# The expert stage as one program: gates of four batches first, shared tiles next, and the routing arithmetic spread over the first tiles

## The chip, the cores and the metric

The kernel runs on one core of a Trainium2 chip. The time is the device time of one execution in microseconds (us). TensorE is called PE here, VectorE DVE, ScalarE ACT, GpSimd POOL and SyncE SP, as the profile does.

## The reference, cut to what matters

The whole program is a small network: five stages of attention and feed-forward, and last a mixture of experts. Only that last stage is touched:

```
logits = x @ gate_w.T                       # x: 4096 normalized rows of 256
scores = softmax(logits)                    # over 8 experts
topk_w, topk_i = top_k(scores, 2)
topk_w = topk_w / (topk_w.sum(-1) + 1e-20) * 2.5
g = silu(x @ w_gate[e]) * (x @ w_up[e])     # 352 wide
expert_out = g @ w_down[e]
y = sum of the two chosen experts' outputs, each times its topk_w
out = y + (silu(x @ sw_gate) * (x @ sw_up)) @ sw_down    # shared network, 704 wide
```

The result is added to the residual rows.

## The kernel before, in words

The stage is the function `stage_expert_ffn`. It holds the 4096 rows as 32 tiles of 128 rows and 256 columns (`NT = 32`, eight tiles to each of four batches, `TB = 8`). It multiplies with 352-wide networks only: the shared network is cut in two halves, A and B. So there are ten networks of `NW = 2176` columns (gate, up and down side by side), each loaded by one DMA and split in a high part (ACT, `split_high`) and a low part (POOL, `split_low`), since every product is made of high times high, high times low and low times high.

It has two programs (Blocks) with a barrier between them.

**The first program** is the routing. SP saves the residual rows to memory and loads the networks. DVE measures and normalizes the rows (`measure`, `apply`). PE turns each batch (16 transposes, L3353) and multiplies it with the gate (32 small products, L3362). Then 40 small operations run on DVE one after the other. Each is a `step`: DVE waits for its own semaphore before it goes on. They make the softmax, pick the two best experts, count the rows of each expert (with two products on PE, L3368 and L3369, and a running sum over the 32 tiles), and give each row its place (`slots`) in a list that is sorted by expert. ACT makes the exponential in between.

**The second program** is a pipeline over `K = 135` tiles of rows: 0 to 31 are the 32 tiles with shared half A, 32 to 102 are 71 tiles of the sorted list with the expert of each (`R0 = 32`), and 103 to 134 are the 32 tiles with shared half B, where the two expert outputs of each row are gathered and added. In iteration i each engine does, in this order:

- PE: turns the rows of tile i+1 (L3571), `up(i)` (12 products, L3594 to L3599), turns the product of tile i-1 (L3606), `down(i-2)` (9 products, L3617 to L3619).
- ACT: `high_x(i+1)` (L3638), in some tiles a whole `split_high` (L3273), silu of tile i (L3664), `hT_high(i-1)` (L3668).
- DVE: `low_x(i+1)` (L3674), adds of tile i-3 (L3682), the product `prod(i)` of silu and up (L3713), `hT_low(i-1)` (L3716). In iteration 0 it makes the last 8 routing steps too (`place_tiles`, `weigh_picks`).
- SP: loads and stores of the kept rows and of the sorted list.

Each waits for the others by semaphores: silu(i) for up(i) and for prod(i-1), up(i) for prod(i-2), and so on, so that a delay of one is soon a delay of all.

In the same time POOL spreads the rows: 64 indirect DMAs (L3539), each of which writes 128 rows to their places in the sorted list. It makes them in eight bursts of eight, and after each burst it splits one network (704 and 1472 columns, L3277). Tile 32 needs all 64 and all splits:

```
for t in range(NT):
    g.wait_ge(upped.sem, upped.at(3 * t // 4))
    for i in range(2):
        g.indirect_dma_start(xs[:, :], ...)
    if t % 4 == 3:
        split_low(g, t // 4 + 1, 0, GU)
        split_low(g, t // 4 + 1, GU, NW)
```

## Time and profile before

| | |
|---|---|
| median of 3 runs | 4069.13 us (4068.13 to 4070.47) |
| the profiled execution | 4078.57 us, its span 4076.8 us |
| granted TensorE clock, mean of the span | 0.928 |
| PE busy | 3499.0 us (86% of the span) |
| DVE busy | 2930.9 us (72%) |
| ACT busy | 2550.4 us (63%) |
| POOL busy | 1863.8 us (46%) |

The shares are means over six stages. The expert stage is the last 597 us of the span (from 3479.9 to 4076.8 us), and what is said below is read in it, but for one stretch of an earlier stage. Times such as 3552.55 are microseconds from the start of the span.

### The profile page before, as it was taken

The numbers are of one execution on the slowest core, as the hardware profiler recorded it, in microseconds if no ns is written. First come the engines' busy times: TensorE is split into PE (matmuls) and PEld (weight loads), VectorE is DVE, ScalarE is ACT, GpSimd is POOL, SyncE is SP. The second block draws the span as 40 slices with busy tenths as digits, with TensorE's granted clock in tenths as the row PEclk, the third lists the DMA queues.
The fourth block names the chain that finished last, engine by engine and source line by source line (L and its number), as shares of the span: only waits on it lengthen the run. The fifth ranks groups of instructions, "written<-read, shape, count | busy, mean of one in ns | idle before, by whom it ended". The sixth has DMA issues, their size and how long they took to land. (4 is left out here: it accounts for less than half of the span.)

```text
span 4076.8 us, 64192 instructions
## 1 busy us (share of the span) xinstructions
PE 3499.0 (86%) x22125; PEld 2796.1 (69%) x22128; DVE 2930.9 (72%) x5974; ACT 2550.4 (63%) x3361; POOL 1863.8 (46%) x1143
## 2 busy tenths in 40 slices
PE   6867623369999999999999999995889889679999
PEld 4645421247777777877778788773767667579999
DVE  4568789868878887788878888884666675434347
ACT  2334445448878887787878878872666666234433
POOL 0034410026555565565555556532766666380005
PEclk9988856689999999999999999996999999699999
DMA  1047700058878888787878878880748559432224
GB/s 49 0 94 131 143 1 1 1 139 151 143 139 147 140 149 140 139 153 139 143 138 142 151 143 155 154 155 18 134 88 152 102 91 176 166 122 90 76 77 144
DMA packets 1571360, 470.22 MB, mean 115 GB/s; under 512 B 1507174, under 2 KB 1565159, under 8 KB 1569767
## 3 DMA queue, kind: packets, MB, share of 16 engines
q1 hardware_dynamic: 1564903, 449.40, 58.0%
q0 software_dynamic: 6144, 16.79, 1.2%
q8 instruction: 179, 2.93, 0.3%
q14 instruction: 134, 1.10, 0.1%
HBM read 49.00 MB, written 39.58 MB: 22 GB/s over the span
## 5 line engine op out<-in xcount | busy, mean ns | idle before, releaser
L2299 DVE TENSOR_REDUCE d_neg_max<-psum 128x1 f32<-128x1024 f32 x512 | 625.1, 1221 | 249.9 <-PE psum L2040 244.1
L2189 ACT ACTIVATE psum<-psum,d_bias 128x1024 f32<-128x1024 f32 x512 | 557.6, 1089 | 336.0 <-DVE d_bias L2303 332.2
L2040 PE MATMUL psum<-d_KH,d_QH 128*128 128x512 f32 x2048 | 682.7, 415 | 19.7 <-DVE d_halves L2308 12.3
L2308 DVE SCALAR_TENSOR_TENSOR d_halves<-psum,d_halves 128x1024 f16<-128x1024 f32 x512 | 623.1, 1217 | 24.9 <-ACT d_halves L2196 22.0
L2040 PE MATMUL psum<-d_KL,d_QH 128*128 128x512 f32 x2048 | 638.1, 393 | 0.0
L2040 PE MATMUL psum<-d_KH,d_QL 128*128 128x512 f32 x2048 | 637.3, 392 | 0.0
L1999 POOL TENSOR_TENSOR d_KC<-d_KC,d_tap_of 128x1024 f32<-128x1024 f32 x126 | 301.9, 2396 | 566.0 <-ACT d_tap_of L2179 566.0
L2196 ACT ACTIVATE d_halves<-psum 128x1024 f16<-128x1024 f32 x512 | 521.8, 1019 | 3.5
L2040 PEld LDWEIGHTS psum<-d_KH,d_QH 128*128 128x128 f32 x2048 | 360.8, 189 | 131.6 <-issue 40.5
L2040 PEld LDWEIGHTS psum<-d_KL,d_QH 128*128 128x128 f32 x2048 | 385.1, 188 | 86.9
L2040 PEld LDWEIGHTS psum<-d_KH,d_QL 128*128 128x128 f32 x2048 | 385.2, 188 | 86.7
L2006 POOL TENSOR_TENSOR d_KL<-d_KC,d_KH 128x1024 fp32r<-128x1024 f32 x128 | 307.9, 2406 | 189.9 <-ACT d_KH L2185 189.9
L2883 POOL TENSOR_TENSOR e_halves<-e_probs,e_halves 128x1102 f16<-128x1102 f32 x128 | 292.5, 2285 | 128.5 <-ACT e_halves L2984 127.2
L1995 POOL TENSOR_TENSOR d_KC<-d_KC,d_tap_of 128x1024 f32<-128x1024 f32 x126 | 307.0, 2436 | 28.0 <-ACT d_tap_of L2179 19.8
L2179 ACT ACTIVATE d_tap_of<-d_K,d_taps 128x1024 f32<-128x1024 f32 x252 | 289.1, 1147 | 0.0
L2054 PE MATMUL psum<-d_probsT,d_V 128*64 128x256 f16 x4096 | 249.1, 275 | 2.2 <-DMA d_probsT<-d_halves 2.2
L2054 PEld LDWEIGHTS psum<-d_probsT,d_V 128*64 128x64 bf16 x4096 | 214.0, 110 | 49.0 <-issue 46.1
L2977 ACT ACTIVATE e_probs<-psum,e_neg_max 128x1102 f32<-128x1102 f32 x128 | 150.3, 1174 | 94.2 <-DVE e_neg_max L3056 94.0
L3713 DVE TENSOR_TENSOR f_prod<-psum,f_silu 128x352 f32<-128x352 f32 x135 | 70.5, 523 | 148.2 <-ACT f_silu L3664 128.1
L3664 ACT ACTIVATE f_silu<-psum 128x352 f32<-128x352 f32 x135 | 62.9, 466 | 174.8 <-PE psum L3599 143.3
L3052 DVE TENSOR_REDUCE e_own_neg_max<-psum 128x1 f32<-128x1102 f32 x128 | 167.1, 1305 | 4.4
L3551 POOL DMA_INDIRECT f_tile<-f_expert_out,f_slots x64 | 60.8, 950 | 236.6 <-DMA f_expert_out<-f_tile 183.8
(513 smaller groups left out, 7606.3 us busy)
## 6 DMA issues: line engine op xcount, KB each, us to landing
f_weights_raw<-in_L_ffn_packed_dram SPq DMA_DIRECT2D x10, 1088.0 KB, 15.9
f_tile<-expert_rows SPq DMA_DIRECT2D x71, 128.0 KB, 2.2
f_expert_out<-f_tile SPq DMA_DIRECT2D x71, 128.0 KB, 1.7
d_probsT<-d_halves SPq DMA_TRANSPOSE x512, 4.3
f_tile<-f_kept_rows SPq DMA_DIRECT2D x64, 128.0 KB
expert_rows<-d_group_mixT SPq DMA_DIRECT2D x7, 1024.0 KB, 11.4
residual_stream<-in_x_dram SPq DMA_DIRECT2D x4, 1024.0 KB, 9.4
f_kept_rows<-residual_stream SPq DMA_DIRECT2D x4, 1024.0 KB, 8.6
```

Of the source, the lines that this page charges most:

```text
L1995: g.tensor_tensor(KC[:, ch, :], KC[:, ch, :], tap_of[:, ch, :], ALU.add)\
L1999: g.tensor_tensor(KC[:, ch, :], KC[:, ch, :], tap_of[:, ch, :], ALU.add)\
L2006: g.tensor_tensor(KL[hh % 2][:, ch, :], KC[:, ch, :], KH[hh % 2][:, ch, :].bitcast(F32), ALU.subtract).then_inc(key_low.sem, 1)
L2040: last = t.matmul(scores_at(u)[:, cols], q_part[:, ch, j * P:(j + 1) * P], k_part[hh % 2][:, ch, cols], start=k == 0, stop=k == 5)
L2054: last = t.matmul(mix_bank[part * WIDE:(part + 1) * WIDE, at:at + 2 * P], V[:, k, h, :], probsT[p % 3][:, part * TB + k, :, :].rearrange(" ...
L2179: a.activation(tap_of[:, ch, :], K[b % 2][:, ch, k:S + k], ACT.Copy, scale=taps[:, ch, 3 * h + k:3 * h + k + 1]).then_inc(tapped.sem, 1)
L2189: a.activation(scores_at(u), scores_at(u), ACT.Exp, bias=bias[u % 2][:, 0:1])\
L2196: a.activation(halves[u % 4][:, 0, :], scores_at(u), ACT.Copy, scale=LIFT)\
L2299: v.tensor_reduce(neg_max[u % 2][:], scores_at(u), AXIS.X, ALU.max, negate=True)\
L2308: v.scalar_tensor_tensor(halves[u % 4][:, 1, :], scores_at(u), LIFT, halves[u % 4][:, 0, :], ALU.mult, ALU.subtract).then_inc(probs_low.se ...
L2883: g.tensor_tensor(halves[i % 3][:, 1, 0:W], probs[i % 3][:], halves[i % 3][:, 0, 0:W], ALU.subtract)\
L3052: v.tensor_reduce(own_neg_max[g % 2][:], scores_at(u), AXIS.X, ALU.max, negate=True)\
```

## The change

The two programs become one. The gates of all four batches come first on PE, now in half batches. Then the pipeline over the tiles begins, and the routing steps, now 38, are made in it by DVE: those of the first choice in iteration 0, of the second in 1, the places in 3 and 4, the experts of the tiles in 8 and the weights in 11. The choice is made from the logits, with no softmax; the two exponentials come in iteration 10 on ACT. The running sum over the tiles is done on PE in `rank_rows`, by 33 products that add up in one bank. POOL makes six whole splits first, waits for the places (27 steps), and then issues all 64 indirect DMAs with nothing between them; it then loads the first three tiles of the sorted list itself. The last two networks are split on DVE, in four pieces in iterations 18 to 24. Up to tile 32 only one bank holds the result of `down`.

```diff
-    EARLY = 3
+    ON_POOL = 6
+    RANKED_AT = 2
...
+        def pick_first(v):
+            step(v, v.tensor_reduce(top[0][:], logits, AXIS.X, ALU.max))
+            step(v, v.tensor_tensor(shifted[:], logits, per_tile(top[0][:]), ALU.subtract))
+            step(v, v.scalar_tensor_tensor(cell[:], shifted[:], 0.0, per_expert(number[:]), ALU.is_equal, ALU.mult))
+            step(v, v.tensor_reduce(top_at[0][:], cell[:], AXIS.X, ALU.min))
+            step(v, v.tensor_tensor(pick[0][:], per_expert(number[:]), per_tile(top_at[0][:]), ALU.is_equal))
+            step(v, v.scalar_tensor_tensor(masked[:], pick[0][:], NEG, shifted[:], ALU.mult, ALU.add))
...
+        def pick_second(v):
+            step(v, v.tensor_reduce(top[1][:], masked[:], AXIS.X, ALU.max))
+            step(v, v.tensor_tensor(lowered[:], masked[:], per_tile(top[1][:]), ALU.subtract))
+            step(v, v.scalar_tensor_tensor(cell[:], lowered[:], 0.0, per_expert(number[:]), ALU.is_equal, ALU.mult))
+            step(v, v.tensor_reduce(top_at[1][:], cell[:], AXIS.X, ALU.min))
+            step(v, v.tensor_tensor(pick[1][:], per_expert(number[:]), per_tile(top_at[1][:]), ALU.is_equal))
+            step(v, v.tensor_tensor(chosen[:, 0:NT, :], pick[0][:], pick[1][:], ALU.add))
...
+        def place_experts(v):
+            v.wait_ge(ranked.sem, ranked.at(1))
+            step(v, v.tensor_tensor(over[:], rank[:, NT, :].unsqueeze(2).to_broadcast([P, E, NT]),
+                                    tile_rows[:].unsqueeze(1).to_broadcast([P, E, NT]), ALU.is_gt))
+            step(v, v.tensor_reduce(tiles[:], over[:], AXIS.X, ALU.add))
+            step(v, v.tensor_copy(ends[0][:, HE:HE + E], tiles[:]))
+            for i in range(3):
+                shift, old, new = 1 << i, ends[i % 2], ends[(i + 1) % 2]
+                step(v, v.tensor_tensor(new[:, HE:HE + E], old[:, HE:HE + E], old[:, HE - shift:HE - shift + E],
+                                        ALU.add))
+            step(v, v.tensor_tensor(first_tile[:], end, tiles[:], ALU.subtract))
+            step(v, v.tensor_scalar(first_row[:], first_tile[:], float(P), None, ALU.mult))
+
...
+        def place_rows(v):
+            step(v, v.tensor_tensor(where[:], rank[:, 0:NT, :], per_expert(first_row[:]), ALU.add))
+            for i in range(2):
+                step(v, v.tensor_tensor(cell[:], pick[i][:], where[:], ALU.mult))
+                step(v, v.tensor_reduce(slot_f[i][:], cell[:], AXIS.X, ALU.add))
+                step(v, v.tensor_copy(slots[:, i, :], slot_f[i][:]))
...
+        route_plan = {0: pick_first, 1: pick_second, 3: place_experts, 4: place_rows, 8: place_tiles,
+                      11: weigh_picks}
+        CHOSEN, PLACED, TILED, STEPS = 12, 27, 30, 38
+        late_split = {18: (ON_POOL + 1, 0, GU), 20: (ON_POOL + 1, GU, NW), 22: (ON_POOL + 2, 0, GU),
+                      24: (ON_POOL + 2, GU, NW)}
+        high_plan = {i: i + 1 for i in range(ON_POOL)}
+        high_plan[16], high_plan[18], high_plan[R0 + 20] = ON_POOL + 1, ON_POOL + 2, E + 1
...
+                save(0)
+                sp.dma_start(gate_w[:], chunked(w["gate_w"])).then_inc(gate_in.sem, 16)
+                load_net(sp, 0)
+                for b in range(1, B):
+                    save(b)
+                for n in range(1, E + 1):
+                    load_net(sp, n)
                 for s in range(K + 3):
...
+                unit_norms(0)
+                unit_norms(1)
+                split_low(g, 0, 0, NW, weight_low)
+                unit_norms(2)
+                unit_norms(3)
...
+                for n in range(1, ON_POOL + 1):
+                    split_low(g, n, 0, NW, weight_low)
                 g.wait_ge(rows_cleared.sem, rows_cleared.at(16 * 8))
+                g.wait_ge(route.sem, route.at(PLACED))
                 for t in range(NT):
-                    g.wait_ge(upped.sem, upped.at(3 * t // 4))
                     for i in range(2):
                         g.indirect_dma_start(xs[:, :], bass.IndirectOffsetOnAxis(ap=slots[:, i, t:t + 1], axis=0),
                                              X[:, t, :], None).then_inc(spread.sem, 16)
-                    if t % 4 == 3:
-                        split_low(g, t // 4 + 1, 0, GU)
-                        split_low(g, t // 4 + 1, GU, NW)
-                split_low(g, E + 1, 0, NW)
+                g.wait_ge(spread.sem, spread.at(16 * 2 * NT))
+                for r in range(3):
+                    g.dma_start(T[3 + r][:], rows(xs, r)).then_inc(x_first[r].sem, 16)
+                split_low(g, E + 1, 0, NW, weight_low)
...
+                def rank_rows():
+                    t.wait_ge(const_built.sem, const_built.at(10))
+                    t.wait_ge(route.sem, route.at(CHOSEN))
+                    flat = chosen[:].rearrange("p t e -> p (t e)")
+                    at = 7 * BANK
+                    t.matmul(PS[:, at:at + (NT + 1) * E], before[:], flat, start=True, stop=False)
+                    for shift in range(1, NT + 1):
+                        last = t.matmul(PS[:, at + shift * E:at + (NT + 1) * E], every[:],
+                                        flat[:, 0:(NT + 1 - shift) * E], start=False, stop=shift == NT)
+                    last.then_inc(ranked.sem, 1)
+
...
-                        t.wait_ge(weight_low.sem, weight_low.at(2 * E + 1))
+                        t.wait_ge(weight_low.sem, weight_low.at(ON_POOL + 1))
+                        t.wait_ge(weight_low_late.sem, weight_low_late.at(len(late_split)))
+                        t.wait_ge(route.sem, route.at(STEPS))
...
-                    y_free(t, k - 2)
+                    y_free(t, k - 1 if k <= R0 else k - 2)
...
+                turn_half(0, 0)
+                turn_half(0, 1)
                 turn_x(0)
+                for b in range(1, B):
+                    gate_half(b - 1, 0)
+                    turn_half(b, 0)
+                    gate_half(b - 1, 1)
+                    turn_half(b, 1)
+                gate_half(B - 1, 0)
+                gate_half(B - 1, 1)
...
+                    if i == RANKED_AT:
+                        rank_rows()
...
+                    if i in high_plan:
+                        split_high(a, high_plan[i])
+                    if i == 10:
+                        a.wait_ge(route.sem, route.at(CHOSEN))
+                        a.activation(scores[:], shifted[:], ACT.Exp).then_inc(route_exp.sem, 1)
+                        a.activation(second_exp[:], top[1][:], ACT.Exp).then_inc(route_exp.sem, 1)
...
+                    if i in route_plan:
+                        route_plan[i](v)
+                    if i in late_split:
+                        split_low(v, *late_split[i], weight_low_late)
```

The first place is POOL's program, from its last operations before the spread on. A row is an operation with the names of what it writes and reads; `f_weights_raw` with a number is a network as loaded, `expert_rows` the sorted list. Before:

```order
L3277 TENSOR_TENSOR f_weights_low<-f_weights_raw_43850,f_weights_high 128x2176
L3539 DMA expert_rows<-residual_stream,f_slots 9088x256 x8
L3277 TENSOR_TENSOR f_weights_low<-f_weights_raw_43842,f_weights_high 128x704
L3277 TENSOR_TENSOR f_weights_low<-f_weights_raw_43842,f_weights_high 128x1472
L3539 DMA expert_rows<-residual_stream,f_slots 9088x256 x8
L3277 TENSOR_TENSOR f_weights_low<-f_weights_raw_43843,f_weights_high 128x704
L3277 TENSOR_TENSOR f_weights_low<-f_weights_raw_43843,f_weights_high 128x1472
```

And now:

```order
L3478 CAST f_pre_before<-f_pre_before_f 128x128
L3281 TENSOR_TENSOR f_weights_low<-f_weights_raw_43842,f_weights_high 128x2176
L3281 TENSOR_TENSOR f_weights_low<-f_weights_raw_43843,f_weights_high 128x2176
L3281 TENSOR_TENSOR f_weights_low<-f_weights_raw_43844,f_weights_high 128x2176
L3281 TENSOR_TENSOR f_weights_low<-f_weights_raw_43845,f_weights_high 128x2176
L3281 TENSOR_TENSOR f_weights_low<-f_weights_raw_43846,f_weights_high 128x2176
L3281 TENSOR_TENSOR f_weights_low<-f_weights_raw_43847,f_weights_high 128x2176
L3485 DMA expert_rows<-residual_stream,f_slots 9088x256 x64
L3489 DMA f_tile_43863<-expert_rows 128x256
L3489 DMA f_tile_43864<-expert_rows 128x256
L3489 DMA f_tile_43865<-expert_rows 128x256
L3281 TENSOR_TENSOR f_weights_low<-f_weights_raw_43850,f_weights_high 128x2176
```

The splits stood behind each eight indirect DMAs (the three rows of a burst come eight times); now six stand ahead of all 64.

The second place is DVE's program around the first product of the tile pipeline. Before (`f_slots` are the places, the last steps of the first program; the rows from `f_pre_passed` on are the steps of iteration 0):

```order
L3464 TENSOR_REDUCE f_pre_slot_f_43914<-f_pre_cell_43891 128x32
L3465 CAST f_slots<-f_pre_slot_f_43914 128x32
L3674 TENSOR_TENSOR f_xT_low_43853<-psum,f_xT_high_43851 128x256
L3674 TENSOR_TENSOR f_xT_low_43854<-psum,f_xT_high_43852 128x256
L3290 TENSOR_TENSOR f_pre_passed<-f_pre_tile_number,f_pre_ends_43908 128x568
L3292 TENSOR_REDUCE f_pre_te_f<-f_pre_passed 128x71
L3293 TENSOR_SCALAR f_tile_expert<-f_pre_te_f 128x71
L3296 TENSOR_TENSOR f_pre_pair_sum<-f_pre_top_43893,f_pre_top_43894 128x32
L3713 TENSOR_TENSOR f_prod_43856<-psum,f_silu 128x352
```

And now, from the last normalized rows on:

```order
L3683 TENSOR_TENSOR f_xT_low_43854<-psum,f_xT_high_43852 128x256
L3303 TENSOR_REDUCE f_pre_top_43891<-psum 128x32
L3304 TENSOR_TENSOR f_pre_shifted<-psum,f_pre_top_43891 128x256
L3305 SCALAR_TENSOR_TENSOR f_pre_cell<-f_pre_shifted,f_pre_number 128x256
L3306 TENSOR_REDUCE f_pre_top_at_43893<-f_pre_cell 128x32
L3307 TENSOR_TENSOR f_pre_pick_43888<-f_pre_number,f_pre_top_at_43893 128x256
L3308 SCALAR_TENSOR_TENSOR f_pre_masked<-f_pre_pick_43888,f_pre_shifted 128x256
L3747 TENSOR_TENSOR f_prod_43856<-psum,f_silu 128x352
L3683 TENSOR_TENSOR f_xT_low_43853<-psum,f_xT_high_43851 128x256
L3311 TENSOR_REDUCE f_pre_top_43892<-f_pre_masked 128x32
L3312 TENSOR_TENSOR f_pre_lowered<-f_pre_masked,f_pre_top_43892 128x256
```

Ahead of the first product stand the six steps of the first choice, and ahead of the second product six more of the second choice; the steps that ended before the pipeline began now stand between its operations.

## Rows read from the trace of the kernel before

**Rows 1.** Timeline of PE: start, length, operation [idle before, releaser]; gates to first tile.

```profile
3519.68 3.65 PE L3353 MATMUL psum<-ident,residual_stream 128*128 128x128 f32 x16
3524.08 4.47 PE L3362 MATMUL psum<-f_pre_gate_w,f_pre_xT 128*128 128x8 f32 x32 [0.75 <-ACT f_pre_xT L3380]
...
3546.71 0.66 PE L3571 MATMUL psum<-ident,residual_stream 128*128 128x128 f32 x2 [9.12 <-PEq L3304]
...
3548.64 0.64 PE L3594 MATMUL psum<-f_weights_high,f_xT_high 128*128 128x352 f32 x1
```

**Rows 2.** Timeline of DVE, first, seventeenth and last routing step of the first program.

```profile
3528.66 0.42 DVE L3422 TENSOR_REDUCE f_pre_lowest<-psum 128x32 f32<-128x256 f32 x1 [23.94 <-PE psum L3362]
...
3536.43 0.42 DVE L3438 TENSOR_TENSOR f_pre_chosen<-f_pre_pick,f_pre_pick 128x256 bf16<-128x256 f32 x1
...
3545.99 0.18 DVE L3465 CAST f_slots<-f_pre_slot_f 128x32 int32<-128x32 f32 x1
```

**Rows 3.** Timeline of ACT in the tile pipeline: first tile.

```profile
3549.43 1.28 ACT L3664 ACT_TABLE_LOAD   x1
3552.55 0.47 ACT L3664 ACTIVATE f_silu<-psum 128x352 f32<-128x352 f32 x1 [1.83 <-PE psum L3599]
...
3553.26 2.01 ACT L3273 ACTIVATE f_weights_high<-f_weights_raw 128x2176 fp32r<-128x2176 f32 x1
```

**Rows 4.** Timeline of ACT, silu of tiles 32 and 33.

```profile
3696.86 0.47 ACT L3664 ACTIVATE f_silu<-psum 128x352 f32<-128x352 f32 x1 [1.81 <-PE psum L3599]
...
3700.41 0.47 ACT L3664 ACTIVATE f_silu<-psum 128x352 f32<-128x352 f32 x1 [1.33 <-PE psum L3599]
```

**Rows 5.** Timeline of PE, the two counting products.

```profile
3537.01 0.37 PE L3368 MATMUL psum<-f_pre_chosen,f_pre_before 128*128 128x256 bf16 x1 [8.46 <-DVE f_pre_chosen L3438]
3537.17 0.42 PE L3369 MATMUL psum<-f_pre_chosen,f_pre_every 128*128 128x256 bf16 x1
```

**Rows 6.** Timeline of POOL: first split, second burst and its splits.

```profile
3526.01 4.78 POOL L3277 TENSOR_TENSOR f_weights_low<-f_weights_raw,f_weights_high 128x2176 fp32r<-128x2176 f32 x1 [22.08 <-ACT f_weights_high L3273]
...
3563.25 0.99 POOL L3539 DMA_INDIRECT expert_rows<-residual_stream,f_slots  x1 [0.17 <-issue]
...
3572.14 0.96 POOL L3539 DMA_INDIRECT expert_rows<-residual_stream,f_slots  x1 [0.30 <-issue]
3573.12 4.96 POOL L3277 TENSOR_TENSOR f_weights_low<-f_weights_raw,f_weights_high 128x704 fp32r<-128x704 f32 x2
```

**Rows 7.** Line L3539 of POOL, all indirect DMAs: least, median, most ns.

```profile
L3539 POOL DMA_INDIRECT expert_rows<-residual_stream,f_slots x64: 957/963/1307, 3547.5 to 3662.2; - x64
```

**Rows 8.** Timeline of ACT, ends of its halts in bursts two to four.

```profile
3571.94 0.46 ACT L3664 ACTIVATE f_silu<-psum 128x352 f32<-128x352 f32 x1 [2.71 <-remote]
3574.91 0.49 ACT L3668 ACTIVATE f_hT_high<-psum 128x384 fp32r<-128x384 f32 x1 [2.51 <-remote]
...
3589.78 0.47 ACT L3664 ACTIVATE f_silu<-psum 128x352 f32<-128x352 f32 x1 [3.92 <-remote]
...
3604.83 0.46 ACT L3664 ACTIVATE f_silu<-psum 128x352 f32<-128x352 f32 x1 [3.50 <-PE psum L3599]
```

**Rows 9.** Timeline of ACT at the eight gathers of half B.

```profile
3962.41 0.38 ACT L3638 ACTIVATE f_xT_high<-psum 128x256 fp32r<-128x256 f32 x1
3969.15 0.47 ACT L3664 ACTIVATE f_silu<-psum 128x352 f32<-128x352 f32 x1 [6.36 <-remote]
```

**Rows 10.** Timeline of POOL, first and last of those eight gathers.

```profile
3957.64 1.00 POOL L3551 DMA_INDIRECT f_tile<-f_expert_out,f_slots  x1 [183.77 <-DMA f_expert_out<-f_tile]
...
3966.96 0.95 POOL L3551 DMA_INDIRECT f_tile<-f_expert_out,f_slots  x1 [0.31 <-issue]
```

**Rows 11.** Timeline of POOL in an earlier stage.

```profile
3108.49 2.29 POOL L2883 TENSOR_TENSOR e_halves<-e_probs,e_halves 128x1102 f16<-128x1102 f32 x1
...
3118.11 2.29 POOL L2883 TENSOR_TENSOR e_halves<-e_probs,e_halves 128x1102 f16<-128x1102 f32 x1
```

**Rows 12.** Timeline of DVE in the same stretch.

```profile
3108.46 2.46 DVE L3087 TENSOR_SCALAR e_ln_xn<-residual_stream,e_ln_mean_var,e_ln_rstd 128x256 f32<-128x256 f32 x1 [2.42 <-POOL e_ln_rstd L2909]
...
3113.42 0.40 DVE L3087 TENSOR_SCALAR e_ln_xn<-residual_stream,e_ln_mean_var,e_ln_rstd 128x256 f32<-128x256 f32 x1
...
3119.28 0.88 DVE L3072 SCALAR_TENSOR_TENSOR residual_stream<-psum,e_inv_sum,residual_stream 128x256 f32<-128x256 f32 x2
```

**Rows 13.** Line L2340 of DVE, two inputs from SBUF: least, median, most ns.

```profile
L2340 DVE TENSOR_TENSOR d_QL<-d_ln_xn,d_QH x32: 410/416/2560, 872.9 to 2304.1; 128x256 fp32r<-128x256 f32 x32
```

More of the change, by code:

```diff
@@ L3158, in stage_expert_ffn @@
     weight_low = c("f_weight_low")
+    weight_low_late = c("f_weight_low_late")
     saved = [c(f"f_saved{b}") for b in range(B)]
@@ L3213, in stage_expert_ffn @@
         hTH, hTL = place("hT_high", [P, 3, P], F32R), place("hT_low", [P, 3, P], F32R)
+        tile_at = [at + 4 * D * i for i in range(7)]
         T = [place(f"tile{i}", [P, D]) for i in range(7)]
@@ new lines, in stage_expert_ffn @@
+        HE = E // 2
+        end = ends[1][:, HE:HE + E]
+        def place_experts(v):
[10 more added lines that the diff above has]
+            step(v, v.tensor_scalar(first_row[:], first_tile[:], float(P), None, ALU.mult))
@@ new lines, in weigh_picks @@
+            for i, prob in enumerate((inv, second)):
+                step(v, v.scalar_tensor_tensor(share[:, i, :], prob[:], SCALE, pair_inv[:], ALU.mult, ALU.mult))
+        route_plan = {0: pick_first, 1: pick_second, 3: place_experts, 4: place_rows, 8: place_tiles,
[3 more added lines that the diff above has]
+                      24: (ON_POOL + 2, GU, NW)}
@@ new lines, in _ @@
+                unit_norms(0)
[3 more added lines that the diff above has]
+                unit_norms(3)
+                g.memset(before_f[:], 1.0).then_inc(const_built.sem, 1)
+                g.memset(every[:], 1.0).then_inc(const_built.sem, 1)
+                g.memset(chosen[:, NT, :], 0.0).then_inc(const_built.sem, 1)
+                for i in range(2):
+                    g.memset(ends[i][:, 0:E // 2], 0.0).then_inc(const_built.sem, 1)
@@ L3557, in _, with turn_half, gate_half @@
                 expert = {}
+                def turn_half(b, u):
+                    t.wait_ge(normed.sem, normed.at(TB * b + 4 * u + 4))
+                    for ch in range(DC):
+                        bank = gate_bank(b, ch)
+                        t.wait_ge(xT_ready.sem, xT_ready.at(4 * b + 2 * u + ch - 1))
+                        for q in range(4):
+                            last = t.transpose(PS[:, bank + q * P:bank + (q + 1) * P],
+                                               X[:, TB * b + 4 * u + q, ch * P:(ch + 1) * P], core.ident[:])
+                        last.then_inc(g_turned.sem, 1)
+                def gate_half(b, u):
+                    if b == 0 and u == 0:
+                        t.wait_ge(gate_in.sem, gate_in.at(16))
+                    t.wait_ge(xT_ready.sem, xT_ready.at(4 * b + 2 * u + 2))
+                    for q in range(4):
+                        col = 7 * BANK + (TB * b + 4 * u + q) * E
+                        for ch in range(DC):
+                            last = t.matmul(PS[:, col:col + E], gate_xT[u][:, ch, q * P:(q + 1) * P],
+                                            gate_w[:, ch, :], start=ch == 0, stop=ch == DC - 1)
+                    last.then_inc(gated.sem, 1)
+                def rank_rows():
[8 more added lines that the diff above has]
+                    last.then_inc(ranked.sem, 1)
                 def turn_x(k):
```

294 lines of the change are left out of this document (102 added, 192 removed).

## Prediction

> **What bounds the kernel now.** I read the page first (which engine is busy), then the timelines of PE, DVE and ACT where the routing ends and the tiles begin, then ACT and POOL through tiles 0 to 32, and last an earlier stage for a case that this one lacks. All times are of the profiled execution (4078.57 us); it lies 9.4 us above the median of the runs, so the forecast is its time less 9.4. A measurement of this kernel can tell some 8 us (0.2%) from no change.
>
> Two stretches of the expert stage are not bound by PE's products. The first is the routing. The last gate product ends at 3524.08 + 4.47 = 3528.55, and up(0) starts at 3548.64 [rows 1]. In between DVE makes 40 steps, the large ones of 0.42 us, from 3528.66 to 3546.17 [rows 2]; nothing else has work, and the reader sees PE's idle 9.12 ahead of its first turn. That is 20.1 us on the path.
>
> The second is tiles 0 to 31. A tile in quiet takes 3.55 us (silu of 32 and 33 [rows 4]), so 32 tiles would take 113.6. From silu(0) at 3552.55 [rows 3] to silu(32) at 3696.86 [rows 4] there are 144.3: 30.7 us are lost. Where they go is seen when ACT is laid beside POOL. POOL's second burst of indirect DMAs starts at 3563.25, its last DMA at 3572.14 (1.27 us apart) [rows 6]. ACT stands idle in its second half and after it, and goes on at 3571.94 and 3574.91 [rows 8], the last 2.8 us after the start of the last DMA, with a releaser that the profile calls remote or that was long done. The third and fourth burst (from 3578.25 and 3593.28) end in the same way at 3589.78 and 3604.83 [rows 8]. The eight gathers of half B show it again: burst from 3957.64, last at 3966.96 [rows 10], and ACT idle from 3962.8 to 3969.15 [rows 9]. So 30.7 us for 64 DMAs [rows 7], 0.48 us each, and the first 5 us of a burst cost nothing. The later gathers of half B, two to a tile, stop nobody, so it is the density of such DMAs that matters.
>
> **The change part by part.**
>
> *Routing off the path: -19.5.* Up(0) now follows the gates. The last gate product is a half batch, but there is a copy more in each half batch, so I leave the end of the gates at 3528.55 (bounds: 5 us earlier, 4 later, a batch's turn or gate of 3.65 and 4.47 [rows 1]). With one turn of 0.66 ahead of it, up(0) starts near 3529.1 and not 3548.64. The 5-us split of network 0 is earlier too, and needs nothing.
>
> *The steps inside the tiles, taken by themselves: +3.6.* Iteration 0 had 8 steps before and has 6; iteration 1 gets 6 (2.8 us), of which DVE's idle time in a tile hides most; 3 and 4 get 8 and 7. What PE itself gets is rank_rows: 33 products with 264, 256, 248 ... 8 columns, 4488 in all. The two counting products of 256 columns start 0.16 us apart [rows 5], so 4488/256 x 0.16 = 2.8 us, on PE between its turn and down(0). Another 0.8 for the rest. Bounds 0 and 9 (all of the 2.8 + 2.8 + 3.1 shown).
>
> *Six splits of POOL behind one another, beside DVE's steps: +14.* Here the trace of an earlier stage speaks. A DVE operation from SBUF to SBUF started at 3108.46 and took 2.46 us; the same took 0.40 at 3113.42 [rows 12]. The long one ends with POOL's TENSOR_TENSOR of 3108.49 + 2.29 [rows 11]; the short one has none beside it. DVE's 0.88-us operations at 3119.28 with one input in PSUM run undisturbed inside another of POOL (3118.11 to 3120.40). For two inputs from SBUF, line L2340 has a median of 416 ns and a most of 2560 [rows 13]. So a DVE step with two inputs in SBUF waits for the POOL operation that is running. Before, the split of 4.78 us at 3526.01 [rows 6] lay ahead of the steps, and the others beside tiles whose DVE operations read PSUM. Now 3 of the 6 steps of iteration 0, 4 of 6 in iteration 1, 4 small ones in 3 and 2 in 4 have two such inputs, and POOL runs splits of 4.96. Network 1 is split high after high_x(1), from 3529.5 to 3531.5 (2.01 us [rows 3]); POOL takes it from 3531.6 to 3536.5. The pick step of iteration 0 comes at 3531.8 and waits 4.7 us; the masked step behind it meets the second split and waits 4.95. The first product moves by 9.6. Then ACT, which waits for that product, has no new high part ready, and POOL rests: iterations 1 to 3 pay little. In iteration 4 the two cell steps meet splits 4 and 5, some 6 us; of these sums 1.6 falls into waits that are there anyway. Bounds: 0 and 25 (five splits of 4.96).
>
> Which steps are hit is the open part, since rows 13 do not name what ran beside. [...]
>
> *One burst of 64 for eight of 8: 0.* The DMAs are as many. At 0.48 us each they cost the same 30.7. Nothing here shows a burst of more than eight, so the bounds are far: one halt for the whole burst, 4.4 us (30.7 over the seven bursts that show one), or ACT stopped from 5 us in until 2.8 after its end. The burst is 63 x 1.27 + 0.96 = 81 us, and this would be 79 us. Between them: releases 2.97 apart [rows 8], two to a tile, give 5.94 for 3.55, 40% of 79 = 32. That is near 30.7, and so is my value.
>
> The Trainium skill, page "SBUF — State Buffer", section "SBUF: two separate sides", has it that a DMA cannot slow a compute operation. By that the bursts stop nobody, the two slower rivals below fall away, and 4070 has their chance. The halts of rows 8 and 9 stand where bursts end, in seven of the eight and in the gathers, and I go by them.
>
> *Where POOL's chain ends.* Places at about 3565, sixth split at 3571.5, DMAs to 3653, landed 2.8 later, three loads: about 3659. Without the pacing by tiles, tile 32 comes on PE at about 3697, so 38 us of cover. If there were no halts, the cover would be 12.
>
> *The rest: +3.* Two exponentials on ACT make two table loads of 1.28 [rows 3] and two operations of 0.42, 3.4 us; ACT is idle over half of a tile, so +1. The two networks on DVE: 2176 columns at 416 ns for 256 [rows 13] are 3.5 us each, in four pieces in tiles where DVE has 1.6 us idle: +2 (0 to 7). The single bank for `down` up to tile 32 costs nothing: the add of tile i-3 comes 2 us ahead of down(i-2) and its wait. SP's order (network 0 ahead of three saves) is hidden while PE has gates to make.
>
> **Sum:** -19.5 + 3.6 + 14 + 0 + 3 = +1.1; 4078.57 + 1.1 - 9.4 = **4070**.
>
> **The rivals.**
>
> *No lock on these steps* (0.19). If the steps run beside the splits as the PSUM ones do, the 14 fall away: 4056. For it: the rows are of other operations, and no step of these shapes ran beside a split. Against it: rows 11 to 13.
>
> *The long burst halts once* (0.16). If the halt is bound to the start or end of a burst, 26 us come back. With the lock tile 32 comes at 3671 and the rest is as before: 4044. Without the lock, 4030, where POOL's chain ends too. For it: each burst ends with one release 2.6 to 2.8 after its last DMA. Against it: in the second burst ACT is let go at 3571.94 and held again till 3574.91, so a halt is not one per burst.
>
> *The long burst stops ACT nearly throughout* (0.17): slower. From 5 us into a burst no signal from PE seems to reach ACT before the burst is over (bursts 3 and 4). Then 75 us or so are lost for 30.7: +44, 4114. It decides against the forecast once more than half of the burst is halt (loss over 40 us). Against it: the release at 3571.94 in the middle of the second.
>
> *In between* (0.14): three releases to a tile, 8.9 for 3.55, 60% of 79 = 47, +17: 4087.
>
> The forecast itself (lock, and the burst at its old price) has 0.34; its own range is 4058 to 4082.
>
> **How the numbers follow.** Faster by over 0.2% (below 4061): both of the first two rivals but a little, and the low end of the forecast, 0.34. Within 0.2%: most of the forecast and the high end of "no lock", 0.26. Slower (above 4077): the two last rivals and the high end of the forecast, 0.40. Range: below 4040 lies half of "halts once" (0.07), above 4104 two thirds of "nearly throughout" (0.12): 4040 to 4104.
>
> **What the profile after would show.** Right: up(0) near 3529; in iteration 0 a DVE step of about 5 us beside a POOL split, silu(1) some 9 us late; POOL's 64 DMAs from about 3572 to 3653, and in that stretch tiles of about 6 us; tile 32 near 3697; PE never waits for the spread. Wrong: steps of 0.42 beside the splits; an ACT idle of tens of us, or quiet tiles of 3.55 in the burst; gates that end after 3533; PE at tile 32 waiting for the three loads. The part most likely to fail is the price of a burst longer than any in the trace.

## The result, and the profile after

The changed kernel takes 4126.04 us (median of 4 runs, 4120.07 to 4134.32) where the kernel before takes 4069.8 (4 runs, 4068.13 to 4071.3). The ratio is 1.0134 with a 95% interval of 1.0117 to 1.0150: slower by some 55 us. The forecast was 4070, its range ended at 4104. The result is above it.

I count from the first `measure` operation of the expert stage on DVE (3479.9 before, 3482.7 after), since the earlier stages move by some us from run to run. "Silu(i)" is the start of ACT's silu of tile i. "Quiet" is 3.55 us a tile, as for tiles 32 and 33 in [rows 4]; "lost" is what a stretch takes beyond that.

| profiled execution, us | before | after | difference | forecast |
|---|---|---|---|---|
| start of stage to silu(0) | 72.6 | 54.8 | -17.8 | -19.5 |
| silu(0) to silu(8), 28.4 in quiet | 37.2 | 48.4, so 20.0 lost | +11.2 | 17.6 lost after |
| silu(8) to silu(32), 85.2 in quiet | 107.1 | 162.9, so 77.7 lost | +55.8 | 30.7 + 3 lost after |
| lost in all, silu(0) to silu(32) | 30.7 | 97.7 | +67.0 | +20.6 |
| silu(32) to silu(134) | 367.8 | 365.3 | -2.5 | 0 |

The first and the last start that the table rests on after the change, from the timeline of ACT (silu(8) stands further down):

```profile
3537.54 0.46 ACT L3673 ACTIVATE f_silu<-psum 128x352 f32<-128x352 f32 x1
...
3748.79 0.47 ACT L3673 ACTIVATE f_silu<-psum 128x352 f32<-128x352 f32 x1 [1.31 <-PE psum L3582]
```

The stage is 46.9 us longer in these two executions, and the spans differ by 49.7. The medians are 56 apart, since the profiled execution lies 8.8 us above this median before and 2.2 above it after.

The first tiles, on DVE (timeline: start, length, operation):

```profile
3536.06 0.42 DVE L3306 TENSOR_REDUCE f_pre_top_at<-f_pre_cell 128x32 f32<-128x256 f32 x1
3536.51 4.92 DVE L3307 TENSOR_TENSOR f_pre_pick<-f_pre_number,f_pre_top_at 128x256 f32<-128x256 f32 x1
3541.47 4.87 DVE L3308 SCALAR_TENSOR_TENSOR f_pre_masked<-f_pre_pick,f_pre_shifted 128x256 f32<-128x256 f32 x1
3546.38 0.52 DVE L3747 TENSOR_TENSOR f_prod<-psum,f_silu 128x352 f32<-128x352 f32 x1
...
3550.79 0.41 DVE L3683 TENSOR_TENSOR f_xT_low<-psum,f_xT_high 128x256 fp32r<-128x256 f32 x1
...
3557.99 0.42 DVE L3325 TENSOR_REDUCE f_pre_tiles<-f_over 128x8 f32<-128x256 f32 x1
...
3558.65 9.77 DVE L3329 TENSOR_TENSOR f_pre_ends<-f_pre_ends 128x8 f32<-128x8 f32 x3
...
3576.07 0.53 DVE L3747 TENSOR_TENSOR f_prod<-psum,f_silu 128x352 f32<-128x352 f32 x1 [1.29 <-ACT f_silu L3673]
```

And POOL beside them:

```profile
3536.31 9.75 POOL L3281 TENSOR_TENSOR f_weights_low<-f_weights_raw,f_weights_high 128x2176 fp32r<-128x2176 f32 x2 [27.30 <-ACT f_weights_high L3277]
3550.69 4.82 POOL L3281 TENSOR_TENSOR f_weights_low<-f_weights_raw,f_weights_high 128x2176 fp32r<-128x2176 f32 x1 [4.63 <-ACT f_weights_high L3277]
3558.63 9.57 POOL L3281 TENSOR_TENSOR f_weights_low<-f_weights_raw,f_weights_high 128x2176 fp32r<-128x2176 f32 x2 [3.12 <-ACT f_weights_high L3277]
3575.77 4.88 POOL L3281 TENSOR_TENSOR f_weights_low<-f_weights_raw,f_weights_high 128x2176 fp32r<-128x2176 f32 x1 [7.57 <-ACT f_weights_high L3277]
```

The reader is to see three things. Each long DVE step has two inputs in SBUF and ends shortly after the split beside it: the second at 3546.34, where POOL's first two splits end at 3546.06. Three additions of 8 columns (0.57 together before) last 9.77, to 3568.42, where the next two splits end at 3568.20. And a DVE operation with an input in PSUM keeps its length beside a split (0.41 at 3550.79, 0.53 at 3576.07). The reductions shown ran ahead of the splits, all but the last 0.17 us of one, and so tell nothing of this.

Then the burst, on ACT:

```profile
3585.92 0.47 ACT L3673 ACTIVATE f_silu<-psum 128x352 f32<-128x352 f32 x1 [1.31 <-PE psum L3582]
3589.73 0.49 ACT L3677 ACTIVATE f_hT_high<-psum 128x384 fp32r<-128x384 f32 x1 [3.35 <-remote]
3591.08 0.38 ACT L3632 ACTIVATE f_xT_high<-psum 128x256 fp32r<-128x256 f32 x1 [0.86 <-remote]
3603.21 0.46 ACT L3673 ACTIVATE f_silu<-psum 128x352 f32<-128x352 f32 x1 [11.74 <-remote]
3633.37 0.49 ACT L3677 ACTIVATE f_hT_high<-psum 128x384 fp32r<-128x384 f32 x1 [29.70 <-remote]
3639.60 0.38 ACT L3632 ACTIVATE f_xT_high<-psum 128x256 fp32r<-128x256 f32 x1 [5.75 <-remote]
...
3670.43 0.46 ACT L3673 ACTIVATE f_silu<-psum 128x352 f32<-128x352 f32 x1 [27.30 <-remote]
```

POOL's 64 indirect DMAs stand between these times (first and last of them, and the loads behind):

```profile
3580.85 1.31 POOL L3485 DMA_INDIRECT expert_rows<-residual_stream,f_slots  x1 [0.20 <-issue]
...
3660.82 0.96 POOL L3485 DMA_INDIRECT expert_rows<-residual_stream,f_slots  x1 [0.30 <-issue]
3663.52 1.70 POOL L3489 DMA_DIRECT2D f_tile<-expert_rows  x3 [1.74 <-DMA expert_rows<-residual_stream,f_slots]
```

From 3585.92 to 3670.43, where silu(10) starts, two tiles go through; 23 would in quiet. The halts of [rows 8] were 2.5 to 3.9 us; here one is 29.7, and the mean clock of the span falls from 0.928 to 0.918. The last halt ends 8.6 us after the last DMA does (3661.78). In the four other profiles with halts and an unbroken run of 64 (b1_one_burst, a2_splits_behind_steps, a3_probes and f1_quarter_rows, all below) it is 8.5 to 9.5 us; behind the burst of [rows 6], which has eight, it was 1.8.

### The profile page after: what moved, and what is told of

Same layout as the page of the kernel before. It is cut to its first block and busy times, and to the rows that moved or that the text cites. A ratio compares the mean times of both kernels' runs of the same rounds, so it can differ in the third digit from the quotient of the medians.

```text
span 4126.5 us, 64235 instructions
## 1 busy us (share of the span) xinstructions
PE 3514.0 (85%) x22156; PEld 2807.7 (68%) x22159; DVE 2951.5 (72%) x5968; ACT 2553.3 (62%) x3364; POOL 1852.3 (45%) x1135
## 5 line engine op out<-in xcount | busy, mean ns | idle before, releaser
L3750 DVE TENSOR_TENSOR f_hT_low<-psum,f_hT_high 128x384 fp32r<-128x384 f32 x135 | 75.2, 557 | 147.0 <-ACT f_hT_high L3677 107.9
L3677 ACT ACTIVATE f_hT_high<-psum 128x384 fp32r<-128x384 f32 x135 | 66.3, 491 | 170.8 <-PE psum L3602 119.7
```

## Experiments

**Apart: two kinds of chips.** The groups of runs fell on different chips. On some the kernel before takes 4070 to 4075 us and its bursts halt ACT as in [rows 8]; on others it takes 4042 to 4046. The kernels of a group share the chip, so a group is compared inside itself. "Halt" is an idle time of ACT that ends late although PE's work for it is long done. First the group of four on a chip with halts (the kernel before: 4074.59).

*One burst in the kernel before.*

```diff
                 for t in range(NT):
-                    g.wait_ge(upped.sem, upped.at(3 * t // 4))
                     for i in range(2):
                         g.indirect_dma_start(...)
-                    if t % 4 == 3:
-                        split_low(g, t // 4 + 1, 0, GU)
-                        split_low(g, t // 4 + 1, GU, NW)
+                for n in range(E):
+                    split_low(g, n + 1, 0, GU)
+                    split_low(g, n + 1, GU, NW)
```

> The kernel before, with only POOL's spread changed: all 64 indirect DMAs in one run without the waits for up(3t/4), and the eight splits behind them. Theory A (length of the run): silu(0) to silu(32) grows from 144.3 by 35 to 50 us, the time is 4105 to 4120. Rival B (fixed cost per DMA): within 8 us of 4069.

Measured: 4120.88 us, ratio 1.0113 (1.0092 to 1.0135); silu(0) to silu(32) takes 188.1 us where it took 144.3. The long burst alone (with the splits that stood between its parts now behind it), without any other part of the change, costs 44 us. Two of its halts, on ACT:

```profile
3618.48 0.46 ACT L3663 ACTIVATE f_silu<-psum 128x352 f32<-128x352 f32 x1 [30.69 <-remote]
3640.96 0.49 ACT L3667 ACTIVATE f_hT_high<-psum 128x384 fp32r<-128x384 f32 x1 [22.02 <-remote]
```

The fixed price per DMA is out.

*The pacing put back in the changed kernel.*

```diff
                 for t in range(NT):
+                    g.wait_ge(upped.sem, upped.at(6 + 3 * t // 4))
                     for i in range(2):
```

> The changed kernel with one wait put back: ahead of each pair of indirect DMAs POOL waits until up(6 + 3t/4) has ended on PE. Theory A (what costs is the length of an unbroken run of indirect DMAs; a halt of ACT now stops POOL too, and so ends itself): silu(8) to silu(32) falls from 162.9 us to between 90 and 115 (85.2 in quiet), the time to 4055 to 4080. Rival B (each of the 64 DMAs costs ACT a fixed time, however they follow): within 10 us of 4126. Rival C (the stop comes from the exponentials and their table loads in iteration 10, which stand inside the halt): within 10 us of 4126 too, and the gap of silu(9) to silu(10) stays tens of us.

Measured: 4073.93 us, ratio 1.0001 (0.9991 to 1.0010), silu(8) to silu(32) 112.0 us. One wait brings back 51 of the 77.7 us. The exponentials (rival C) are no cause: with the halts short, the two tiles around iteration 10 take 4.3 and 2.5 us, and b1_one_burst has its long halts with no exponential near them.

*The splits behind the routing steps.*

```diff
+                g.wait_ge(route.sem, route.at(PLACED))
                 for n in range(1, ON_POOL + 1):
                     split_low(g, n, 0, NW, weight_low)
                 g.wait_ge(rows_cleared.sem, rows_cleared.at(16 * 8))
-                g.wait_ge(route.sem, route.at(PLACED))
```

> The changed kernel, with POOL's wait for the 27 steps moved from behind the six splits to ahead of them, so that no split runs beside a routing step. Lock theory: the steps at L3307, L3308 (4.9 us each) and L3329 (9.8 us for three) fall to 0.42, 0.42 and 0.6; silu(0) to silu(5) falls from 38.0 us by 18 to about 20; the burst of 64 costs what it cost (75 us), the time is about 4108. Rival: the long steps are due to something else in those tiles (the clock, PE's weight loads, semaphores): they stay long, 4126.

Measured: 4108.92 us, ratio 1.0091 (1.0069 to 1.0114) where the change has 1.0134. Silu(0) to silu(8) takes 29.5 us, not 48.4. The same steps in its timeline of DVE:

```profile
3527.43 0.42 DVE L3307 TENSOR_TENSOR f_pre_pick<-f_pre_number,f_pre_top_at 128x256 f32<-128x256 f32 x1
3527.89 0.43 DVE L3308 SCALAR_TENSOR_TENSOR f_pre_masked<-f_pre_pick,f_pre_shifted 128x256 f32<-128x256 f32 x1
...
3540.21 0.57 DVE L3329 TENSOR_TENSOR f_pre_ends<-f_pre_ends 128x8 f32<-128x8 f32 x3
```

So the splits beside the steps cost 18.9 us; the steps and `rank_rows` by themselves cost tiles 0 to 8 29.5 - 28.4 = 1.1 us. The burst is dearer here than expected: silu(8) to silu(32) takes 171.4 us, 86.2 lost and not 75. So the price of an unbroken run of 64 is not one number: 74.5 us are lost in all in b1_one_burst, 77.7 in the changed kernel.

*Probes: who is late?*

```diff
                         a.activation(silu[:], g_bank(i), ACT.Silu).then_inc(silu_ready.sem, 1)
+                        if 5 <= i < 14:
+                            a.wait_ge(product.sem, product.at(i + 1))
+                            a.activation(probe[:, i:i + 1], core.ident[:, 0:1], ACT.Copy)
...
+                    if 5 <= i < 14:
+                        v.wait_ge(upped.sem, upped.at(i + 1))
+                        v.tensor_copy(probe[:, 32 + i:33 + i], core.ident[:, 0:1])
```

> The changed kernel with two small copies a tile added in tiles 5 to 13: one on DVE that waits for up(i) of PE ahead of prod(i), one on ACT behind silu(i) that waits for prod(i) of DVE. Theory A1 (signals from PE are late, whoever waits): in the burst DVE's probe starts many us after the end of up(i), as silu does; ACT's probe starts at once behind prod(i). Theory A2 (ACT is held at its waits, whoever signals): DVE's probe starts within 0.3 us of the end of up(i), and ACT's probe is late by us. The time is not looked at (some 5 us more than 4126 by the added work).

The timeline of tile 9 in the burst (the last product of up(9) on PE, then DVE and ACT):

```profile
3582.66 0.32 PE L3583 MATMUL psum<-f_weights_high,f_xT_low 128*128 128x352 f32 x1
...
3593.23 0.42 PE L3583 MATMUL psum<-f_weights_high,f_xT_low 128*128 128x352 f32 x1 [1.10 <-issue]
...
3598.20 0.46 ACT L3674 ACTIVATE f_silu<-psum 128x352 f32<-128x352 f32 x1 [12.44 <-remote]
3598.20 0.15 DVE L3750 COPY f_probe<-ident 128x1 f32<-128x1 f32 x1 [11.66 <-remote]
3598.70 0.53 DVE L3754 TENSOR_TENSOR f_prod<-psum,f_silu 128x352 f32<-128x352 f32 x1 [0.34 <-issue]
3599.26 0.20 ACT L3677 ACTIVATE f_probe<-ident 128x1 f32<-128x1 f32 x1 [0.59 <-DVE f_prod L3754]
...
3664.12 0.15 DVE L3750 COPY f_probe<-ident 128x1 f32<-128x1 f32 x1 [29.70 <-remote]
```

PE ends up(9) at 3582.98 by the trace. ACT and DVE, which wait for that one signal independently, both start at 3598.20, 15.2 us later. ACT's wait for DVE's product is released at once (3598.70 + 0.53, then 3599.26). PE was not slow with up(9): by 3593.65 it had ended up(10) too, the second of its rows above, and ACT and DVE had still seen no signal of up(9). What is late is the signal from PE, whoever waits for it (A1); ACT is not slow (A2 falls). The next one is later still: DVE's probe of tile 10 waits for up(10) alone and starts at 3664.12, 70.5 us after that product's end. (The run takes 4125.34 us.)

**On chips without halts.** The next three groups fell on other chips: the kernel before took 4044.46, 4046.35 and 4042.53 us. The first of them tried where a cure lies. In the mixed kernels POOL waits for the places, then mixes DMAs and splits (here for fours; the pairs have 2 for 4 and 8 for `m // 4`), and DVE makes four networks instead of two. `PART` is 544 columns for fours and 272 for pairs:

```diff
                 for t in range(NT):
                     for i in range(2):
                         g.indirect_dma_start(...)
+                    if (2 * t + 2) % 4 == 0:
+                        m = (2 * t + 2) // 4 - 1
+                        n, lo = m // 4, m % 4 * PART
+                        split_low(g, n + 1, lo, lo + PART, weight_low)
...
+        late_split = {12: (5, 0, GU), 13: (5, GU, NW), 14: (6, 0, GU), 15: (6, GU, NW),
+                      18: (7, 0, GU), 20: (7, GU, NW), 22: (8, 0, GU), 24: (8, GU, NW)}
```

> The changed kernel with POOL's and DVE's shares of the low parts rearranged: POOL waits for the 27 steps first, then issues the indirect DMAs in pairs with a piece of 272 columns of a split behind each pair (32 pieces, four networks); DVE makes the other four networks in eight pieces in iterations 12 to 24. Theory A (unbroken runs hold PE's signals; two DMAs in some 3.3 us do not): no halts, silu(0) to silu(32) between 125 and 145 (bounded by POOL: 17 to the places, 105 for DMAs and pieces, some 8 behind), the time 4045 to 4060. Rival B (any 64 DMAs at this density hold them): silu(0) to silu(32) of 160 or more, 4070 or more.

> As the kernel with pairs, but four indirect DMAs and then a piece of 544 columns (16 pieces). POOL's work is nearly the same, the run of DMAs without a break 5.0 us. Theory A with the onset at 5 us: as the pairs within 8 us, since the runs end when the hold would begin. Theory A with any break needed to be as long as the run: halts of 1 to 3 us in each of the sixteen, 20 us above the pairs.

Measured: pairs 4048.38, ratio 1.0007 (0.9995 to 1.0019), silu(0) to silu(32) 139.4 us; fours 4040.23, 0.9987 (0.9977 to 0.9996), 135.4. No halts, which tells nothing of a cure, since this turned out to be a chip without them. PE waits for POOL's list at tile 32, 22.1 us with pairs and 15.2 with fours. Two more runs changed what is sent, one line for the other:

```diff
-  g.indirect_dma_start(xs[:, :], ..., X[:, t, :], None)
+  g.indirect_dma_start(narrow[:, :], ..., X[:, t, 0:64], None)      # quarter rows
+  g.dma_start(rows(xs, 2 * t + i), X[:, t, :])                      # plain
```

> The changed kernel with the 64 indirect DMAs writing only the first 64 of each row's 256 columns, to another tensor in memory (so the sorted list is not filled, and the rows of the experts are not the reference's). As many DMAs and descriptors, a quarter of the bytes. If the bytes in flight hold PE's signals: the halts go, silu(8) to silu(32) near 90 us, the time some 4055. If it is the making of the DMAs on POOL or their descriptors: the halts stay, silu(8) to silu(32) near 160, 4120.

> The changed kernel with the 64 indirect DMAs replaced by 64 plain ones of the same source tiles and size, from the same POOL queue, to fixed rows of the sorted list (which is then not sorted: the outputs are not the reference's). If the bytes in flight or the queue hold PE's signals: the halts stay. If it is the indirect form, whose descriptors POOL makes itself: no halts, silu(8) to silu(32) 85 to 95, the time near 4050.

Both show 86 us from silu(8) to silu(32). It looked like two answers, and was none: the kernel before was 30 us faster as well, so the chip might have no halts at all. The next group settled that:

> The kernel before, unchanged, for its profile on the same chip as the next three. The last group ran on another chip than the group ahead of it, where the kernel before took 4044 and not 4070 to 4075 us. Theory D (the hold of PE's signals depends on the chip): where the kernel before takes about 4044, its silu(0) to silu(32) is near 120 us without halts; where it takes about 4070, it is 144 with them. Rival (the earlier stages differ by 25 us between chips): 144 on either, and the start of the stage moves.

> The changed kernel, unchanged, beside it. Theory D: on a chip where the kernel before has its halts, 211 us from silu(0) to silu(32) and a ratio of 1.013; on a chip where it has none, about 134 us and a ratio of 1.000 to 1.002 (17.8 us gained ahead of silu(0), 20.0 lost in tiles 0 to 8).

On this chip (the kernel before 4046.35) the unchanged kernel before takes 122.6 us from silu(0) to silu(32), not 144.3, and the changed one 138.7, not 211.3. Its time is 4044.48, ratio 0.9988 (0.9974 to 1.0002), a little under the 1.000 to 1.002 expected. From the start of the stage to silu(0) the two take 75.1 and 54.9 us, so about 20 us are gained there and 16 given back up to tile 32. The same burst of 64 is there, and ACT goes on (timeline of the changed kernel, burst from 3576.33 to 3659):

```profile
3592.04 0.46 ACT L3673 ACTIVATE f_silu<-psum 128x352 f32<-128x352 f32 x1 [0.60 <-PE psum L3582]
3594.02 0.49 ACT L3677 ACTIVATE f_hT_high<-psum 128x384 fp32r<-128x384 f32 x1 [1.51 <-PE psum L3602]
3594.40 0.38 ACT L3632 ACTIVATE f_xT_high<-psum 128x256 fp32r<-128x256 f32 x1
3596.09 0.46 ACT L3673 ACTIVATE f_silu<-psum 128x352 f32<-128x352 f32 x1 [1.31 <-PE psum L3582]
```

There the kernel before waits for POOL's list at tile 32 (PE, from its timeline):

```profile
3664.40 0.69 PE L3571 MATMUL psum<-ident,f_tile 128*128 128x128 f32 x2 [8.57 <-DMA f_tile<-expert_rows]
```

Theory D holds as far as these runs go: the same two kernels have halts in one group of runs and none in another, and the earlier stages do not explain it (silu(0) of the kernel before is at 3550.2 here, 3552.6 there). In the five groups of experiments, on five chips, the median of the kernel before was 4042 to 4046 or 4070 to 4075 us, with nothing between. But no chip was used for two groups, so that it is a lasting property of the chip, and not of the hour or of what surrounds the run, is not shown. "A chip with halts" is meant so from here on. The other two of this group, and the four of the next, were meant for a chip with halts and fell on chips without (the last on one where the kernel before takes 4042.53):

> The changed kernel with the indirect DMAs writing 64 of the 256 columns to another tensor, again (the sorted list is not filled). If this chip has halts in the unchanged kernel, this run tells what the first one could not: silu(8) to silu(32) near 90 if the bytes matter, near 160 if only the number of DMAs does. On a chip without halts it is near 86 either way.

> Four indirect DMAs, then a piece of 544 columns, again. On a chip with halts: theory A (a run of 5 us ends before the hold begins) 135 to 142 us from silu(0) to silu(32) and a ratio to the kernel before of 0.993 to 0.995; if runs of four are held as well, 155 or more and a ratio of 0.998 or more. On a chip without halts a ratio of 0.9985 as before.

> The changed kernel with the indirect DMAs writing 64 of the 256 columns to another tensor (the sorted list is not filled), a third time, for a chip on which the kernel before has its halts (told by the time of the kernel before: near 4070, not 4045). There: if the bytes of the DMAs hold PE's signals, silu(8) to silu(32) is near 90 us; if their number or their making does, near 160.

> The changed kernel with 64 plain DMAs of the same tiles from POOL's queue (the list is not sorted), again. On a chip with halts: silu(8) to silu(32) near 86 if the indirect form is needed for a halt; over 100 if 8.4 MB from POOL's queue do it in any form.

> Four indirect DMAs, then a piece of 544 columns, a third time, for a chip with halts. There: ratio to the kernel before 0.992 to 0.995 if a run of four ends before the hold begins; 0.998 or more if not. On a chip without halts 0.999 as before.

Quarter rows 90.0 and 87.9 us from silu(8) to silu(32), plain DMAs 86.1: on such a chip they tell nothing. Fours 0.9994 (0.9983 to 1.0005) and 0.9995 (0.9982 to 1.0007). With pieces of 544 columns fours were never run on a chip with halts. New in that group was a lighter load for POOL (`PART` of 272 columns, two networks; DVE has six in twelve pieces):

> Four indirect DMAs, then a piece of 272 columns (16 pieces, two networks on POOL), six networks on DVE in twelve pieces in iterations 6 to 24. POOL's chain is 10 us shorter than with pieces of 544 columns, so the wait of tile 32 for the sorted list falls from 20 to about 10 us. On a chip without halts: ratio to the kernel before 0.996 to 0.998. On a chip with halts, if breaks of 0.9 us are enough: 0.990 to 0.993; if not, some 1.00.

Measured: ratio 0.9989 (0.9974 to 1.0003), silu(0) to silu(32) 130.7 us, the wait of PE for the list 11.84. That ratio is above the 0.996 to 0.998 expected: silu(0) to silu(32) is 4 us shorter than with the heavier load, but the time is not shorter beyond the interval.

**Again on a chip with halts.** The last two fell on a chip where the kernel before takes 4070.02 us.

> The changed kernel with the indirect DMAs writing 64 of the 256 columns to another tensor (the list is not filled), once more for a chip with halts (the kernel before near 4070 us). There: silu(8) to silu(32) near 90 us if the bytes hold PE's signals, near 160 if the number of DMAs does. On a chip without halts 86 to 90, which tells nothing.

Measured: 4124.19 us; silu(8) to silu(32) 160.8. In its burst the queues move 30 GB/s (DMA view of 3590 to 3650), against 114 in the changed kernel:

```profile
DMA packets 1793, 1.81 MB, mean 30 GB/s; under 512 B 784, under 2 KB 1040, under 8 KB 1792
```

and ACT is held as long as with whole rows:

```profile
3613.97 0.46 ACT L3674 ACTIVATE f_silu<-psum 128x352 f32<-128x352 f32 x1 [24.90 <-remote]
3647.63 0.49 ACT L3678 ACTIVATE f_hT_high<-psum 128x384 fp32r<-128x384 f32 x1 [33.20 <-remote]
```

So it isn't the bytes. What is left is the indirect DMAs as such, their number, or how POOL makes them. Plain DMAs were never run on a chip with halts, so that the indirect form is needed is not shown.

> Four indirect DMAs, then 272 columns, six networks on DVE, again. On a chip with halts: a ratio to the kernel before of 0.990 to 0.993 if breaks of 0.9 us behind runs of 5 us are enough, near 1.00 if not. On a chip without halts 0.999 as before.

Measured: 4040.34 us, ratio 0.9915 (0.9885 to 0.9944), silu(0) to silu(32) 129.8 us. 16 us in all are lost beyond quiet, and the longest halt is 3.6 us:

```profile
3649.66 0.46 ACT L3676 ACTIVATE f_silu<-psum 128x352 f32<-128x352 f32 x1 [3.56 <-remote]
```

Its 64 DMAs with the 16 pieces take 101 us where the unbroken run takes 81. Of the 81 us that it saves up to tile 32 against the changed kernel (211.3), some 19 are the splits that no longer run beside the steps (silu(0) to silu(8) takes 29.5 us); the other 62 are the broken burst. This version beats the kernel before and the changed one on a chip with halts, and on one without (0.9989) it is where the changed kernel is (0.9988).

## Why the prediction was wrong

**The step that failed** is "One burst of 64 for eight of 8: 0", the same 30.7 us at 0.48 us each. By the profile, tiles 8 to 32 lose 77.7 us. B1_one_burst shows such a price with only POOL's order changed (+43.8 us up to tile 32, 46 in the medians). The loss is not proportional to the DMAs: a burst costs little in its first 5 us and nearly all of the time after. The rival "stops ACT nearly throughout" was this case, with 75 us for 30.7 and 4114; it had 0.17. I weighed against it by the release at 3571.94, called it one in the middle of the burst, and took two releases 2.97 us apart as a rate that would go on. It is not in the middle: it comes 8.7 us into a burst that lasts 9.9. In the long burst ACT's waits were 3.4, 0.9, 11.7, 29.7, 5.8 and 27.3 us: no steady rate, and three of them far longer than any of [rows 8]. Two points of a short burst were no ground for a rate. The range left that rival two thirds out.

**How the 56 us of the miss add up.** The profiled time was forecast as 4079.7 and is 4128.2, 48.6 more. Nearly all of it is found: 44.0 for silu(8) to silu(32), 2.4 for silu(0) to silu(8), 1.7 ahead of silu(0), -2.5 behind tile 32, and 2.8 by which the stage starts later. The other 7.2 are the term -9.4, which was to lead from the profile to the median and was -2.2. That part has nothing to do with the change.

**Routing off the path:** right. 17.8 for 19.5 us. The missing 2 us are the gates: first turn to last gate product takes 42.5 us after and 40.4 before. PE ran them at 1.2 GHz (granted clock 0.50 in the windows from 3490 to 3530, PE busy without a gap from 3494.3), while before it had stretches with a mean of 0.67 and 0.70. Two windows of the changed kernel, and one of the kernel before:

```profile
3500.00:3510.00 10.00, 10.00 (x49) 10.00 (x49) 9.85 (x35) 2.39 (x4) 4.58 (x13) 0.50 1.02 425
3510.00:3520.00 10.00, 10.00 (x49) 10.00 (x49) 0.45 (x2) 2.39 (x4) 0.00 (x0) 0.50 1.01 420
...
3500.00:3510.00 10.00, 9.25 (x55) 8.86 (x54) 4.72 (x13) 2.77 (x5) 3.79 (x12) 0.67 1.01 423
```

(stretch, its us, busy time of PE, its weight loads, DVE, ACT, POOL, then granted clock, DMA share, GB/s). Why it got none of the higher stretches isn't shown.

**Splits beside the steps:** right in kind, 18.9 us for 14. The first two waits were as forecast (4.92 and 4.87). The other two I put in iteration 4, on the `cell` steps; they came in iteration 3, on the additions of 8 columns, since the splits were released later than I laid them out (the first at 3536.31, not 3531.6), and cost 9.2. One row was read wrongly: L3087 of [rows 12] has one full input in SBUF (the other two are a value per row), so it showed that a DVE operation can wait for POOL, but not that two SBUF inputs are the condition. And the 0.88 at 3119.28 are two operations of 0.44.

The Trainium skill, page "SBUF — State Buffer", section "Who interferes with whom", says that a VectorE instruction with two SBUF inputs contends with a GpSimd instruction that reads SBUF. That held here: 4.92 and 4.87 us with two such inputs, 0.41 and 0.53 with one of them in PSUM. The Trainium skill has on the same page, section "SBUF: two separate sides", that a DMA cannot slow a compute operation. The halts do not touch that: the silu in the burst kept its 0.46 us, and a signal came later. Nor did the 4070 follow that I drew from it: bursts that stop nobody would have given the 30.7 us back as well.

**The steps by themselves:** 1.1 us for 3.6, up to tile 8. `rank_rows` and the steps fall for the most part into waits.

**The rest:** about 1 for 3. On a chip without halts the tiles around the exponentials take 5.4 + 1.7 = 7.1 us, which is two quiet tiles, the next two 4.1 each (the last routing steps stand in iteration 11), and in the changed kernel the tiles with DVE's splits (20 to 24) stay at 3.55.

**POOL's chain** had cover while there were halts. Without halts it is late: one gap of 7.6 us ahead of silu(31) in the changed kernel, 4 more than in quiet, and two of 14.2 and 4.2 in the kernel before. I had it as 12 us of cover without halts, where my own numbers, 38 less 30.7, give 7; and the sixth split ended at 3580.65 and not at 3571.5.

**What no profile at hand could show** is that the price of the change differs from one group of runs to another: 1.3% slower with halts, no difference that can be told from none without (0.9988, 0.9974 to 1.0002). Of the 30.7 us that I read as the kernel's, 21.7 are gone in the group without halts (122.6 for 144.3). The 9.0 that remain come with the wait for POOL's list.

## What to carry to other kernels

Don't let GpSimd issue indirect DMAs in an unbroken run beside a tight pipeline on PE: four at a time, with a piece of other work (most of them 0.8 us) between them, went with 16 us lost up to tile 32, where unbroken runs of 64 lost 75 to 86 us. On a chip without halts neither order changed the time by more than 0.2%, so measure the unchanged kernel beside the changed one on the same chip. Before work is moved beside a long GpSimd operation, look at which VectorE operations have both inputs in SBUF. And do not scale a stall by a count when the trace has it at one length only.

## What the runs showed of the hardware

- During a run of indirect DMAs, on some chips, a signal of PE reaches ACT and DVE late: 15.2 and 70.5 us after the end of the product in the probes (a3_probes), up to 33.2 us in one wait (f1_quarter_rows). DVE to ACT is prompt in the same run (0.03 us after the product at 3599.23). A quarter of the bytes changes nothing (160.8 us for 162.9, silu(8) to silu(32)). Which part of the path holds the signal stays open.
- On other chips the same program shows no such wait in 80 us of burst (4044.48 us for 4126.04; silu(8) to silu(32) 90.4 us for 162.9). Whether it is the chip itself is not shown.
- A DVE addition of 8 columns beside a POOL split lasts until the split's end (three of them 9.77 us, against 0.57). With one input in PSUM a DVE operation keeps its length (0.41 at 3550.79).
